# The prologue of a sparse-attention and expert kernel, rebuilt: what leads on TensorE, what is projected late, who makes the rotary tables, and in how many loads the weights come

## The reference, cut to what matters

```python
c_kv = x @ W_dkv;  c_q = x @ W_dq
q_i = (x @ idx_wq)                      # 4 index heads of 64
k_i = x @ idx_wk
I   = sum_h idx_w[h] * relu(q_i[h] @ k_i.T)   # local keys +inf, later keys -inf
idx = top_k(I, 96)
key_c = (c_kv @ W_uk)[idx];  value = (c_kv @ W_uv)[idx]
query_c = c_q @ W_uq
query_r = pope(c_q @ W_qr, angles_q)          # softplus, then rotation
key_r   = pope((x @ W_kr)[idx], angles_k)     # angle by rank in the list
attn = softmax((query_c @ key_c + query_r @ key_r) * scale) @ value @ W_out
```

## Time and profile before

| | |
|---|---|
| median of 3 executions | 851.15 us (849.14 to 852.13) |
| profiled execution | 852.38 us |
| its span | 850.3 us |
| TensorE busy | 786.4 us, 92% |
| VectorE busy | 651.8 us, 77% |
| ScalarE busy | 510.2 us, 60% |
| GpSimd busy | 494.1 us, 58% |
| moved by DMA | 39.95 MB |

### The profile page before, as it was taken

The page is one execution under the profiler, slowest core; times in us unless marked ns, Lnnn a source line. Parts: engine busy times, 40 slices in busy tenths (PEclk is TensorE's granted clock), DMA queues, the critical chain, the costliest instruction groups (busy, mean ns, idle before and its releaser), DMA issues.

```text
span 850.3 us, 17278 instructions
## 1 busy us (share of the span) xinstructions
PE 786.4 (92%) x5702; PEld 470.6 (55%) x5702; DVE 651.8 (77%) x1924; ACT 510.2 (60%) x1463; POOL 494.1 (58%) x510
## 2 busy tenths in 40 slices
PE   5869999999999999999999999899989888999986
PEld 3324555656666565655656566566669344545543
DVE  1978977979899998979899999942322469786964
ACT  5445557767688778787887786686514144254330
POOL 3177777777776777777777776777610615202210
PEclk9856959999999999999999999999979999999999
DMA  8411322222111111111111111138226100000000
GB/s 252 94 22 32 62 39 48 34 51 42 28 32 28 26 32 26 30 31 25 32 31 26 29 30 23 32 92 214 65 85 182 43 7 1 0 1 13 13 1 25
DMA packets 59638, 39.95 MB, mean 47 GB/s; under 512 B 27840, under 2 KB 50592, under 8 KB 59424
## 3 DMA queue, kind: packets, MB, share of 16 engines
q1 hardware_dynamic: 42528, 21.83, 10.1%
q0 software_dynamic: 14336, 15.72, 9.9%
q10 hardware_dynamic: 2688, 1.31, 0.6%
HBM read 33.31 MB, written 5.55 MB: 46 GB/s over the span
## 4 chain that ended last, share of the span: by engine, by line
PE 65%; DVE 15%; ACT 8%; issue 7%; DMA 2%; POOL 2%; SPq 0%; POOLq 0%; ACTq 0%; DVEq 0%
PE psI L654 8%; PE psK L640 6%; PE psP L806 4%; ACT R L902 4%; PE psS L780 3%; PE psK L732 3%; PE psK L744 3%; PE psP L813 3%; PE psP L795 3%; PE psS L783 3%; PE psS L1753 3%; PE psP L640 2%; PE psS L823 2%; DVE top L1142 2%; PE psM L717 2%
## 5 line engine op out<-in xcount | busy, mean ns | idle before, releaser
L623 POOL DMA_INDIRECT G<-key_rows,idx x320 | 320.8, 1003 | 124.9 <-issue 94.2
L654 PE MATMUL psI<-kiT,qiT 64*128 64x512 f32 (+5 forms) x320 | 91.8, 600 | 14.3 <-ACT R L902 14.1
L640 PE MATMUL psK<-cst 128*128 128x512 bf16 x339 | 96.9, 394 | 0.0
L1030 ACT ACTIVATE PT<-psP 128x256 f32<-128x256 f32 x128 | 48.5, 379 | 74.6 <-PE psP L813 72.4
L1114 DVE SCALAR_TENSOR_TENSOR SC<-R,w_i,SC 128x512 f32<-128x512 f32 (+5 forms) x120 | 78.4, 654 | 5.2 <-ACT R L902 2.4
L902 ACT ACTIVATE R<-psI 128x512 f32<-128x512 f32 (+5 forms) x160 | 73.4, 510 | 11.6 <-PE psI L654 9.9
L1142 DVE MAX8 top<-SC 128x8 f32<-128x128 f32 (+15 forms) x64 | 78.4, 1225 | 2.4
L1144 DVE FIND_INDEX8 idxf<-top,SC 128x8 uint32<-128x128 f32 (+15 forms) x64 | 78.2, 1222 | 0.0
L1006 ACT ACTIVATE KT<-psK 96x512 f32<-96x512 f32 x108 | 63.9, 591 | 22.3 <-PE psK L732 21.2
L1545 POOL TENSOR_SCALAR rstd<-mv 128x4 f32<-128x4 f32 x12 | 3.1, 257 | 121.1 <-DVE mv L1949 121.1
L998 ACT ACTIVATE PR<-PR,rinv 128x208 f32<-128x208 f32 x128 | 58.5, 457 | 24.2 <-DVE rinv L1316 22.8
(11 more groups left out here) (352 smaller groups left out, 1730.0 us busy)
## 6 DMA issues: line engine op xcount, KB each, us to landing
G<-key_rows,idx POOLq DMA_INDIRECT x320, 2.5
rtmp<-idx_rows SPq DMA_DIRECT2D x20, 128.0 KB, 3.2
xslots<-zrow SPq DMA_DIRECT2D x4, 320.0 KB, 9.4
SC<-xslots SPq DMA_DIRECT2D x8, 160.0 KB, 2.5
yslots<-SC ACTq DMA_DIRECT2D x8, 160.0 KB, 2.7
V<-val_rows SPq DMA_DIRECT2D x15, 80.0 KB, 2.1
xr<-in_x SPq DMA_DIRECT2D x1, 1024.0 KB, 9.4
qiT<-in_w_gate SPq DMA_DIRECT2D x4, 256.0 KB, 3.9
```

Of the source, the lines that this page charges most:

```text
L623: pool.indirect_dma_start(ring[o % RING][:, g % GPB, DR:], None, key_rows, bass.IndirectOffsetOnAxis(ap=idx[:, t, g:g + 1], axis=0),).then ...
L640: pe.matmul(ps[:, :].rearrange("p (a n) -> p a n", a=2), warm_w, warm_x, start=True, stop=True, skip_group_check=True)
L654: pe.matmul(psI[i][:, 0:w], lhs, kiT[64 * i:64 * i + 64, CH * c:CH * c + w], start=True, stop=True).then_inc(s["i_mm"], 1)
```

## The change

What leads on TensorE: nine products of zeros, then chunk 0's projection, tile 0's index scores, the first half of the key rows, tile 1's scores, the second half, with two products of zeros in between; then the weight products, tile 2's scores, tile 0's query product, and chunk 1. Chunks 2 and 3 stand in the loop, at `n == -NB + 2` and `n == -NB + 4`. ScalarE's copies follow the same order. GpSimd makes all tables, `rank_tab` and the rotated local keys; the factor `-SCALE` is put into the angle instead of a pass over `rot`. Seven weights are one tensor `w_x`, loaded by ScalarE's queue; four are `W_first`; `cst` comes in three parts. TensorE, still in the prologue, before and after:

```diff
-    for t in range(2, NT):
+    for t in range(3, NT):
...
-                sp.dma_start(w_idxk[:, 0:DH], dram["idx_wk"]).then_inc(s["ld_w"], 16)
-                sp.dma_start(w_idxk[:, DH:P], dram["idx_wk"]).then_inc(s["ld_w"], 16)
                 sp.dma_start(xT[:, 0:CH], dram["xT"][:, 0:CH]).then_inc(s["ld_x"], 16)
-                sp.dma_start(w_idxq[:, :], dram["idx_wq"]).then_inc(s["ld_w"], 16)
...
                 sp.dma_start(raw[:, :], dram["raw"]).then_inc(s["ld_raw"], 16)
+                sp.dma_start(tab[:, :, :, :], dram["tab"]).then_inc(s["ld_tab"], 16)
                 sp.dma_start(xT[:, CH:], dram["xT"][:, CH:]).then_inc(s["ld_x2"], 16)
...
+                sp.dma_start(cst[:, C_IM:C_TRI], dram["cst"][:, C_IM:C_TRI]).then_inc(s["ld_cst"], 16)
+                sp.dma_start(w_first[0:DH, :], dram["W_first"]).then_inc(s["ld_late"], 16)
...
-                rotary_angles(pool, link, QF[:, 0:4, :].rearrange("p a (b f) -> p (a b) f", f=HALF).rearrange(
-                    "p (a t) f -> p a t f", a=2), (2, 0))
+                rotary_angles(pool, link, turn, 2)
+                rotary_angles(pool, link, turn, 0)
+                rotary_angles(pool, link, turn, 1)
+                pool.wait_ge(s["ld_late"], 16 * 6)
...
+                    link(pool.tensor_tensor(rank_tab[:, k, :, :], turn[:, 0, 0:2, :], turn[:, 1, 0:2, :], op))
+                pool.wait_ge(s["mu"], 4)
...
+                def zero_products(count):
+
+                    for _ in range(count):
+                        pe.matmul(psP[:, :], zrow[:, 0:P // 2].bitcast(BF16), zrow[:, 0:CH // 2].bitcast(BF16),
+                                  start=True, stop=True, skip_group_check=True)
+
+                pe.wait_ge(s["zeroed"], 1)
+                zero_products(WARM_FIRST)
...
+                project(0)
+                for u in range(2):
+                    index_pair(0, u)
+                    zero_products(WARM_GAP)
+                pe.wait_ge(s["ld_x2"], 16)
+                key_products(0)
...
-                    if n == -NB - 1:
-                        q_project(0)
+                    if n == -NB + 2:
+                        pe.wait_ge(s["lT_cp"], NT // 4)
+                        project(2)
+                    if n == -NB + 4:
+                        project(3)
...
+                act.dma_start(w_x[:, :], dram["w_x"]).then_inc(s["ld_w"], 16)
...
-                projected(0)
+                projected(0, range(3))
+                for u in range(2):
+                    relu_pair(0, u)
+                projected(0, range(3, 4))
...
+                link(dve.tensor_scalar(dlt[:, 8:10, :], dlt[:, 6:8, :], -SCALE, None, ALU.mult))
...
                 for i in range(TOP_STEPS):
                     topk_step(0, i)
-
-                dve.wait_ge(s["ld_late"], 16 * 7)
...
+                    if i == 5:
+                        key_min()
+                key_max()
+                dve.wait_ge(s["ld_late"], 16 * 6)
```

More of the change, by code:

```diff
@@ L423, in load_experts, with rotary_angles @@
                              dram[w][EG * k:EG * (k + 1)].rearrange("e h f -> h e f")).then_inc(s_we[k % NEW], 16)
[L425 to L434, removed]
+        def rotary_angles(eng, link, tmp, k):
+            at = 6 if k == 2 else 8
+            cd = dlt[:, at:at + 1, 0:HALF].to_broadcast([P, NT, HALF])
+            sd = dlt[:, at + 1:at + 2, 0:HALF].to_broadcast([P, NT, HALF])
+            c, sn = tab[:, 2 * k, :, :], tab[:, 2 * k + 1, :, :]
+            for dst, a, b, op in ((2 * k, c, sn, ALU.subtract), (2 * k + 1, sn, c, ALU.add)):
+                link(eng.tensor_tensor(tmp[:, 0, :, :], a, cd, ALU.mult))
+                link(eng.tensor_tensor(tmp[:, 1, :, :], b, sd, ALU.mult))
+                link(eng.tensor_tensor(rot[:, dst, :, :], tmp[:, 0, :, :], tmp[:, 1, :, :], op))
         def proj_banks(c):
@@ L690, in _ @@
                 mm.then_inc(s["w_mm"], 1)
+                for u in range(2):
+                    index_pair(2, u)
                 for j in range(2):
@@ L919, in _, with projected @@
                 act.preload_act_table_set("natural_log_exp_and_others")
-                def projected(c):
-                    for i, (dst, rows) in enumerate(((kiT[:, :], P), (qiT[:, 0, :], P), (qiT[:, 1, :], P),
-                                                     (cqT[:, :], CQ))):
+                def projected(c, parts):
+                    for i in parts:
+                        dst, rows = ((kiT[:, :], P), (qiT[:, 0, :], P), (qiT[:, 1, :], P), (cqT[:, :], CQ))[i]
                         act.wait_ge(s["kproj"], 4 * c + i + 1)
@@ L929, in projected @@
                         act.activation(to, src, ACT.Copy).then_inc(s["kproj_cp"], 1)
-                projected(0)
+                projected(0, range(3))
+                for u in range(2):
+                    relu_pair(0, u)
+                projected(0, range(3, 4))
+                for u in range(2):
+                    relu_pair(1, u)
                 for h in range(2):
@@ L944, in _ @@
                         act.activation(dst[:, 8 * h:8 * h + 8, lat:lat + CKV], src, ACT.Copy).then_inc(s["lat_row"], 1)
-                    if dst is grow:
-                        for u in range(2):
-                            relu_pair(0, u)
-                for u in range(2):
-                    relu_pair(1, u)
-                for c in range(1, CHUNKS):
-                    projected(c)
                 act.wait_ge(s["w_mm"], 1)
@@ L958, in _ @@
                                    ACT.Copy).then_inc(s["w_cp"], 1)
+                projected(1, range(4))
                 def q_softplus(t):
@@ L1084, in _ @@
                                            ACT.Copy).then_inc(s["lT_cp"], 1)
+                    if n in (-NB + 2, -NB + 4):
+                        projected(2 if n == -NB + 2 else 3, range(4))
                     if 0 <= st + 1 < NT:
@@ L1248, in g_rotate @@
                     o = ring_order(n)
+                    if n == 0:
+                        dve.wait_ge(s["rope_p"], 24)
                     if o < FIXED:
```

156 lines of the change are left out of this document (71 added, 85 removed).

## The result

The changed kernel took 839.87 us (median of 4, 835.89 to 843.54) against 850.14 for the kernel before (median of 4): ratio 0.988, 95% interval 0.985 to 0.990. A second comparison of the same two, six executions against eleven, gave 0.982 (0.978 to 0.986). Over both, the medians are 836.9 of ten and 850.5 of fifteen: 13.6 us faster, 1.6%.

What follows compares the result with a forecast made beforehand. The long part runs at TensorE's pace and moves with the prologue's end: 12.6 us at tile 4's sums plus 1.0 behind make 13.6 off 852.4, 838.8, less 1.2 for the median, said as 838 us; range 831 to 845.

Steps and rivals of the forecast that it cites:

- Step 1: Loads and first scores: merged loads and ScalarE's earlier angle chain start VectorE's first sum at 11.5 us, 10.0 us earlier.
- Step 2: Up to the second index list: tables leave VectorE, tile 1's list ready at 30.2 us instead of 43.5, 13.3 us earlier.
- rival B: GpSimd's thirty operations slow VectorE's searches or are slowed, list or local keys 6 us later; 841 to 844 us, 16 in 100.
- rival D: VectorE stands before tile 1 for the late loads, so the gain doesn't arrive; 849 to 853 us, 6 in 100.
- Step 3: First queries: VectorE's waits for scores, queries and softplus go, rotated queries at 40.8 us instead of 58.8.
- Step 4: Moved chunks 2 and 3 come due before tile 4's scores: its first sum at 54.5 us, 12.6 us earlier than 67.12.
- Step 5: First blocks behind tile 4's sums: an earlier clock rise wins at most about 1.5 us, taken as 1.0; the rest unchanged.
- rival C: More than planned: TensorE's low-clock spell at 109 to 127 us shortens, up to 8.9 us gain; 829 to 835 us, 10 in 100.
- Rival E: Slower: the low-clock spell after the first hot blocks lasts longer, 27 us more undo 13.6 us; 855 us, 6 in 100.

Runs made afterwards that it cites:

- raw_first: Changed kernel with the 8.5 KB load of the angles' raw numbers ahead of the first chunk of xT in SP's queue; ratio to before 0.993.
- tables_vector: Changed kernel with table 1, the rank table and the rotated local keys back on VectorE behind tile 0's list; 842.2 us, ratio to before 0.990.
- spell_fill: Changed kernel with 12 more warm products on TensorE ahead of block 4 and 5 ahead of block 10's one-hot products; run twice, ratios to before 0.987 and 0.995.
- no_zeros: Changed kernel without the zero products ahead of the first projection and after the first pairs; 843.6 us, ratio to before 0.986.
- chunks_early: Changed kernel with chunks 2 and 3 projected directly behind chunk 1, ahead of the loop, as before; 842.5 us, ratio to before 0.989.

## Why the prediction was right

It said 838.0 us, 831 to 845; measured 839.9, and 836.9 over ten executions. The forecast's mechanism, the long part moves with the end of the prologue, is what the milestones show. Two things in it were luck: errors of opposite sign in steps 2 to 4 left the sum where it was, and half of the measured gain goes with TensorE's clock, to which the forecast gave only 1.0 us behind the prologue and a middle of two ends in it.

- **Step 1** had the first sum at 11.5; it came at 12.83. The term that was off is the landing of the raw angles, taken as 4.3 us with 4.9 at the latest, and measured 5.9. The weights landed at 5.5 us, not 4.9, and the angles behind them, 4.7 us after their issue; at the head of the queue, in raw_first, they were there by 2.96. The chain behind them took 3.16 us, as reckoned. raw_first moved it and got 1.0 of the 1.3 us back. What the step said of zeros, that they matter little because ScalarE is later, held more fully than its 1.3 us: 0.4 us.
- **Step 2** had the second list at 30.2, and it was there at 30.17, by two errors of opposite sign. Tile 0's list with the minimums, maximums and copy ended 1.5 us late, the lateness of the first sum. The surcharge of 1.7 us for tile 1's sums beside GpSimd didn't come: they took 1.31 us for three, since at 23 us GpSimd was at its six small operations. The rest of tile 1 took its old time but for the conversion of its list (0.48 us instead of 0.18). The searches took 0.29 us beside GpSimd's tables, which refutes rival B; GpSimd finished at 29.9 instead of 28.1, because it began at 8.8 us instead of 7.5 and the small operations took 0.38 us each; the large ones took the 0.78 reckoned. VectorE passed the wait for the late loads without a pause: rival D didn't happen. The table and key operations, which the step counts as seventeen, were nineteen, in the same 7.6 us; tables_vector put eighteen of them back, where its expectation says 28.
- **Step 3** had the rotated queries at 40.8, measured 44.1. Its failing sentence is that the waits go: one of 2.01 us for tile 3's scores and one of 1.08 us for the soft-plus were left. The low clock from 22 to 32 us put chunk 1's projection at 28.0 to 33.7 us instead of 25.4 to 28.9. spell_fill, with the clock high, had neither of them, and 40.6 us.
- **Step 4** had tile 4's first sum at 54.5 with ends 50.8 and 58.4. Measured 54.67 and 54.55. The middle was hit by luck. Chunks 2 and 3 ran at the high clock throughout, for which the step's own sum gives 50.8; 3.3 of the 3.9 us above that are step 3's lateness, from the low spell ahead of them. With the clock high from the start, in spell_fill, it was 50.5. No run showed the low end, both chunks at half clock.
- **Step 5 and rival C.** Behind tile 4's sum 3.8 us were gained, where step 5 had 1.0. The rest is rival C's: the spell of 17 us at 109 to 126 became one of 6.8 at 97 to 104. So the profiled execution, 835.9, lies between the forecast and C. What stands behind tile 4's sum took 779 to 787 us in the six profiles of the first two comparisons, with 14 us of half clock up to 127 us in the shortest and 34 in the longest: some 0.37 us for each us of it, or 0.28 if two short spells behind 700 us, which only the longer has, are counted too.
- **Rival E** priced that at 0.5 and so put the point where the gain is lost at 27 us more of the low clock; by 0.37 it is 37, by 0.28 it is 49. No execution came near it.

The parts show what the prediction had not said: tables and chunks stand side by side in the prologue, and the tables alone gave a wait in place of what they saved. The sum over steps holds for the whole change, not for its parts.

## What to carry to other kernels

When a prologue hands over to a long bound stage, follow a milestone at which the low-clock spells of the start are over. Here that is tile 6's list: against the changed kernel it moved by 15.2, 6.9, 5.4 and 5.7 us (before, no_zeros, tables_vector, chunks_early), and the span by 16.2, 7.7, 6.0 and 6.3. Tile 4's first sum, the forecast's milestone, moved by 12.4, 0.2, 3.7 and 5.2. In a chain over four engines ask of each removed piece what waits behind it on the other engines: the tables of this change, put in alone, bought a wait. Before crediting an edit with a microsecond or two, look where the low-clock spells lie in both profiles; 12 us of spread in this kernel went with them. And compare executions at the same mean clock: here that left half of the gain.

## What the runs showed of the hardware

- TensorE's first products ran at half rate although the granted clock in the windows reads 1.00 there: nine zero products took 3.71 us (0.41 each; ten such products took 4.45 us at the low clock in spell_fill and 2.33 at the high one in the changed kernel), the four projection products behind them 1.98 us; as the first work of the engine the same four took 3.75. The Trainium skill ("TensorE: Matmul & The Clock Gate", What's actually happening) says that the throttled state is the default and activity releases it. The durations agree, the profile's clock column doesn't show it.
- A wait of 1.4 us on TensorE ahead of the same instructions was followed by 10 us at 1.2 GHz in one profile (0.50 granted from 22 to 32 us), by 7 us in a second and by none in a third. The waits of 1.25 and 1.67 us at 106 us stood ahead of the long spell of before, and the same two, at 94 and 96 us, ahead of one of 6.8 us after.
- Beside GpSimd's table operations, VectorE's mask addition took 0.70 us instead of 0.29, the sums of 128 columns 0.75 each, the conversion of the list (CAST, 128x32) 0.54 instead of 0.18, and the searches the 0.28 or 0.29 that they always take. The Trainium skill ("GPSIMD Engine Reference", Key points) names two SBUF inputs and a 2-port mode; the trace agrees for the sums, the mask and the searches; why the conversion slows isn't shown.
- The same kernel before took 850 us in the first two comparisons and 1229 and 1227 us in the last two, on two other chips, with the standstills shown above. Whether that is the chip or its state at the time isn't shown.
